# Decay matrices of a gated delta kernel: rows spread over the partitions by a DMA and subtracted on VectorE, in place of two-row products on TensorE

## The chip, the cores and the metric

The kernel runs on one core of a Trainium2 chip. The metric is the device time in microseconds (us) of one execution; lower is better. The core has TensorE (PE in the profile, with PEld for its weight loads), VectorE (DVE), ScalarE (ACT), GpSimd (POOL), and SyncE (SP), which here issues nearly all DMAs. The engines run beside each other, each through its own instructions in order, and wait for each other at semaphores.

## The reference, cut to what matters

The program is a network of two layers on 1024 tokens of width 256. The part that matters is the attention of the first layer: a gated delta rule with 16 key heads and 32 value heads, two per key head, 128 wide.

```python
beta = jax.nn.sigmoid(b)
g = -jnp.exp(A_log)[None, None, :] * jax.nn.softplus(a + dt_bias[None, None, :])
def step(state, xs):
    q_t, k_t, v_t, g_t, b_t = xs
    state = state * jnp.exp(g_t)[..., None, None]
    kv = jnp.einsum('bhk,bhkv->bhv', k_t, state)
    delta = (v_t - kv) * b_t[..., None]
    state = state + jnp.einsum('bhk,bhv->bhkv', k_t, delta)
    out = jnp.einsum('bhk,bhkv->bhv', q_t, state)
```

The kernel computes this in chunks of 128 tokens. Within a chunk the token pair (j, i), j before or at i, is weighed by exp(G_i - G_j), where G is the running sum of g over the chunk. This is the decay matrix, 128x128, one for each chunk and value head: 8 x 2 = 16 of them for a key head. It is zero where j is after i. The rest of the program (a small MLP, a second attention, a mixture of 32 experts) is not touched.

## The kernel before

The function `heads` runs the first attention as a software pipeline: step h of `STEPS` (0 to 17) prepares key head h + 1 (projection p0 to p7, the convolution's base and taps, silu, key products kk0 and kk1), builds head h (decay matrices, attention products attn0/attn1, the inverse of a triangular 128x128 matrix for each of its 16 pairs of chunk and value head), scans head h - 1 over its 8 chunks (for each chunk c: ks, qs, tx, o, su on PE; x, s, g on VectorE; qs, dl, dt, sq on ScalarE), and finishes head h - 2 (normalisation, output products out0 to out3).

The order of the work is written out by hand for each engine: `PE_PLAN`, `ACT_PLAN`, `DVE_PLAN`, `SP_PLAN` and `POOL_PLAN` hold one step as a row of names, with rows of their own for the first steps (`_FIRST`, `_SECOND`). Every engine goes through its row in order. In PE's row `p3/-1:0` is the first half of projection 3; `z0/2:1` is the second half of z0 into PSUM bank 2. The plans rest on what each piece of work waits for:

- Decay matrices: `gate_rows(h)` (L583 to L586) brings 2 x 16 rows of the running sums and their negatives from DRAM (`cum_rows`) to eight partitions of `row_from` and `row_to`, 16 KB in all, where the second of each pair of partitions or the first holds ones. `decay0` on PE (L855 to L861) makes 16 products over two partitions, which give G_i - G_j for all 16 matrices in four PSUM banks, in 32 passes. VectorE's `decay0` to `decay3` (L1348 to L1350) take min(difference, `limit`) from PSUM to `Dm`, 128x512 each; `limit` is 0 where j is at or before i and -1e30 elsewhere. ScalarE's `exp0` to `exp3` (L1082 to L1087) take the exponential in place. `attn0`, `attn1` (L1351 to L1357) and `inverse0`, `inverse1` (L1285 to L1290) multiply by `Dm`.
- Inverse: GpSimd's `solve` (`eliminate`, L1503 to L1523) inverts the 32x32 diagonal blocks by some 62 small instructions over 29 us. SP's `inverse_out` stores the result (L664 to L669), `inverse_in` loads it back with other partitions (L670 to L674). VectorE's `turn` (L1278 to L1283, three transposes) waits for that load. `y6a` on PE (L887 to L894), the first product that uses it, waits for two of the three transposes; it is a series of 32x64 products at L891 and L892. y6b, u6a, u6b, y7 and u7 follow it.
- Layout changes through DRAM, all issued by SP: `values_out` (4 stores, after VectorE's second transpose of the values, `vt1`) and `values_in` (1024 KB), `kt_out` and `kt_in` for the keys, `products_out` and `products_in` for the key products (after ScalarE's `kk1`), `outputs_out0`, `outputs_in0`, `outputs_out1`, `outputs_in1` for the outputs (after VectorE's `ot0`, `ot1`). Each load waits until its stores have landed. `w_in`, `w_z`, `w_o` bring weights.
- Scan: tx waits for x (VectorE), ks of the next chunk for s (VectorE), o for dl (ScalarE). Chunk 0 needs no x; `s0` waits for su0.
- On GpSimd `pow` and `q_root` are powers of 16 and 8 numbers per partition (2.9 and 1.6 us); `norm0` to `norm3` wait for VectorE's `factors`.

## Time and profile before

| | us |
|---|---|
| median of 3 runs | 1398.15 |
| lowest and highest run | 1395.53, 1399.49 |
| the profiled execution | 1400.72 |
| its span (first to last instruction) | 1398.9 |

| engine | busy us | share of the span |
|---|---|---|
| PE | 1289.0 | 92% |
| PEld | 875.8 | 63% |
| DVE | 969.0 | 69% |
| ACT | 790.9 | 57% |
| POOL | 753.2 | 54% |

The heads stage takes about the first 945 us: a start of some 100 us, 15 steps of about 56 us, and two steps without new heads. The page cuts the span into 40 slices and gives busy tenths for each; 9 is 90% or more:

```profile
PE   6859999999999999999999999898997899499993
PEld 3347767677677676776776767666454566346672
DVE  5848888888888888888888888755222565441554
ACT  3546867677777676777766767654322554210220
POOL 1675886867767868677677686810000000144463
PEclk9869999999999999999999999998998999699997
```

A slice is 35 us. Slices 3 to 26 are the steady steps. Matmuls are pipelined and their ends are modelled, so what one costs is read from the start of one to the start of the next. Shares of the whole span mix stages; what a change in the steps is worth is read from one step.

### The profile page before, as it was taken

The numbers are of one execution on the slowest core, as the hardware profiler recorded it, in microseconds if no ns is written. First come the engines' busy times: TensorE is split into PE (matmuls) and PEld (weight loads), VectorE is DVE, ScalarE is ACT, GpSimd is POOL, SyncE is SP. The second block draws the span as 40 slices with busy tenths as digits, with TensorE's granted clock in tenths as the row PEclk, the third lists the DMA queues.
The fourth block names the chain that finished last, engine by engine and source line by source line (L and its number), as shares of the span: only waits on it lengthen the run. The fifth ranks groups of instructions, "written<-read, shape, count | busy, mean of one in ns | idle before, by whom it ended". The sixth has DMA issues, their size and how long they took to land. (4 is left out here: it accounts for less than half of the span.)

```text
span 1398.9 us, 24967 instructions
## 1 busy us (share of the span) xinstructions
PE 1289.0 (92%) x8680; PEld 875.8 (63%) x8680; DVE 969.0 (69%) x1922; ACT 790.9 (57%) x1947; POOL 753.2 (54%) x1245
## 2 busy tenths in 40 slices
PE   6859999999999999999999999898997899499993
PEld 3347767677677676776776767666454566346672
DVE  5848888888888888888888888755222565441554
ACT  3546867677777676777766767654322554210220
POOL 1675886867767868677677686810000000144463
PEclk9869999999999999999999999998998999699997
DMA  2425355474464553744646537462007900122587
GB/s 87 113 74 118 101 146 142 98 183 118 109 170 110 153 134 97 180 114 125 166 111 154 133 95 179 116 201 68 0 1 304 275 1 1 68 72 94 125 187 186
DMA packets 233180, 171.71 MB, mean 123 GB/s; under 512 B 163746, under 2 KB 202998, under 8 KB 230240
## 3 DMA queue, kind: packets, MB, share of 16 engines
q1 hardware_dynamic: 226912, 161.59, 43.6%
q0 software_dynamic: 6144, 8.53, 3.4%
q8 instruction: 70, 1.15, 0.3%
q14 instruction: 54, 0.44, 0.1%
HBM read 104.64 MB, written 65.83 MB: 122 GB/s over the span
## 5 line engine op out<-in xcount | busy, mean ns | idle before, releaser
L723 PE MATMUL psum_banks<-main_hT,gdn_w_in 128*128 128x512 f32 x512 | 255.2, 609 | 7.4 <-DMA gdn_w_in<-in_w_in 4.1
L1227 DVE SCALAR_TENSOR_TENSOR heads_y<-psum_banks,gdn_conv_w,heads_y 128x1021 f32<-128x1021 f32 (+2 forms) x192 | 244.7, 1275 | 21.7 <-ACT heads_y L1033 17.5
L1522 POOL TENSOR_TENSOR heads_XT<-heads_XT,heads_tmp 128x126 f32<-128x126 f32 (+22 forms) x496 | 198.6, 400 | 38.9
L1519 POOL TENSOR_TENSOR heads_tmp<-heads_XT,heads_A 128x126 f32<-128x126 f32 (+22 forms) x496 | 189.6, 382 | 41.5 <-PE psum_banks L902 1.8
L723 PEld LDWEIGHTS psum_banks<-main_hT,gdn_w_in 128*128 128x128 f32 x512 | 93.5, 194 | 62.1 <-issue 52.7
L849 PE MATMUL psum_banks<-heads_w_z,main_hT 128*128 128x256 f32 x512 | 128.8, 384 | 0.0
L871 PE MATMUL psum_banks<-heads_ogT,heads_w_o 128*128 128x512 f32 x240 | 126.4, 609 | 0.2 <-issue 0.2
L849 PEld LDWEIGHTS psum_banks<-heads_w_z,main_hT 128*128 128x128 f32 x512 | 95.2, 191 | 25.2 <-issue 14.4
L1033 ACT ACTIVATE heads_y<-psum_banks,gdn_conv_w 128x1024 f32<-128x1024 f32 x64 | 71.3, 1114 | 69.3 <-PE psum_banks L723 69.0
L1057 ACT ACTIVATE heads_O<-psum_banks,heads_coef 128x128 f32<-128x128 f32 x224 | 69.6, 363 | 70.5 <-PE psum_banks L756 70.3
L1490 POOL TENSOR_TENSOR heads_og<-heads_og,heads_fac 128x512 f32<-128x512 f32 x60 | 61.2, 1041 | 80.1 <-DVE heads_fac L1294 80.1
L1248 DVE SCALAR_TENSOR_TENSOR heads_S<-heads_S,heads_coef,psum_banks 128x128 f32<-128x128 f32 x192 | 57.3, 339 | 67.9 <-PE psum_banks L773 67.8
L1933 POOL TENSOR_TENSOR main_x<-main_x,attn_probT 128x512 f32<-128x512 f32 x4 | 5.1, 1266 | 150.2 <-ACT attn_probT L1830 150.2
L767 PEld LDWEIGHTS psum_banks<-heads_X,heads_Uf 128*128 128x128 f32 x448 | 66.6, 192 | 29.2 <-issue 15.2
L1076 ACT ACTIVATE heads_junk<-heads_og 128x128 f32<-128x128 f32 x256 | 79.2, 309 | 8.6 <-DVE heads_og L1261 1.2
L753 PE MATMUL psum_banks<-heads_S,heads_kT 128*128 128x256 f32 x224 | 73.7, 411 | 5.8 <-DVE heads_S L1248 3.8
L1239 DVE SCALAR_TENSOR_TENSOR heads_X<-psum_banks,heads_coef,heads_v_s 128x128 f32<-128x128 f32 x224 | 67.9, 345 | 14.9 <-PE psum_banks L753 12.3
L2234 POOL DMA_INDIRECT expert_sum<-moe_ys,moe_place x32 | 49.4, 1542 | 51.0 <-DVE moe_ys L2312 47.8
L1061 ACT ACTIVATE heads_Dl<-psum_banks 128x256 f32<-128x256 f32 x128 | 49.0, 383 | 43.3 <-PE psum_banks L767 43.1
L767 PE MATMUL psum_banks<-heads_X,heads_Uf 128*128 128x128 f32 x448 | 69.5, 278 | 1.9 <-DVE heads_X L1239 1.9
L1065 ACT ACTIVATE heads_Dt<-psum_banks,heads_coef 128x128 f32<-128x128 f32 x224 | 70.5, 375 | 0.0
L753 PEld LDWEIGHTS psum_banks<-heads_S,heads_kT 128*128 128x128 f32 x224 | 37.3, 189 | 52.4 <-DVE heads_S L1248 27.6
(295 smaller groups left out, 3026.4 us busy)
## 6 DMA issues: line engine op xcount, KB each, us to landing
values_by_tokens<-heads_v_s SPq DMA_DIRECT2D x64, 256.0 KB, 4.2
heads_v_s<-values_by_tokens SPq DMA_DIRECT2D x16, 1024.0 KB, 5.1
outputs_by_features<-heads_ogT SPq DMA_DIRECT2D x120, 128.0 KB, 2.4
heads_ogT<-outputs_by_features SPq DMA_DIRECT2D x30, 512.0 KB, 3.8
main_w_gu<-in_w_gu SPq DMA_DIRECT2D x4, 2816.0 KB, 21.0
gdn_w_in<-in_w_in SPq DMA_DIRECT2D x16, 512.0 KB, 4.3
heads_A<-kk_blocks SPq DMA_DIRECT2D x64, 128.0 KB, 2.7
keys_by_tokens<-heads_k_tok SPq DMA_DIRECT2D x64, 128.0 KB, 4.2
```

Source lines behind the costliest of these rows:

```text
L723: ins = pe.matmul(out[:, half * 512:(half + 1) * 512], w_in[:, kd_, j * P:(j + 1) * P], hT[:, kd_, half * 512:(half + 1) * 512], start=kd_ ...
L753: pe.matmul(flat(bank_a[:, 0:2]), kT[(h - 1) % 3][:, cs], flat(S[:]), start=True, stop=True).then_inc(a_full.sem, 1)
L767: ins = pe.matmul(bank_a[:, e], Uf[old][:, e * C + c], rhs, start=True, stop=True)
L849: ins = pe.matmul(flat(bank[b][:, 2 * j:2 * j + 2]), hT[:, k, c * P:(c + 1) * P], w_z[:, k], start=k == 0, stop=k == KD - 1)
L871: ins = pe.matmul(flat(bank[b][:]), w_o[:, e, f], ogT[:, u // 2].rearrange("p q (c e) j -> p e c q j", e=HD)[:, e], start=e == 0, stop=e = ...
L1033: act.activation(y[j][:], out, ACT.Copy, scale=conv_w[:, head, j, 3:4]).then_inc(pair_base.sem, 1)
L1057: ins = act.activation(O1[:, e], bank_b[:, e], ACT.Copy, scale=coef[:, GAM, h - 1, i:i + 1])
L1065: ins = act.activation(Dt[:, e], bank_a[:, e], ACT.Copy, scale=coef[:, TAIL, h - 1, i:i + 1])
L1076: act.activation(junk[:], og[(h - 1) % 2][:, c * HD + e], ACT.Square, accum_out=ms[:, c * HD + e:c * HD + e + 1]).then_inc(sq_ready.sem, 1)
L1227: dve.scalar_tensor_tensor(y[j][:, shift:T], src[:, 0:T - shift], conv_w[:, head, j, t:t + 1], y[j][:, shift:T], ALU.mult, ALU.add).then_i ...
L1519: pool.tensor_tensor(tmp[:, 0:n, 0:m], bc_last(XT[:, 0:n, j], m), bc_mid(A0[:, j, j + 1:BLK], n), ALU.mult).then_inc(solve_step.sem, 1)
L1522: pool.tensor_tensor(XT[:, 0:n, j + 1:BLK], XT[:, 0:n, j + 1:BLK], tmp[:, 0:n, 0:m], ALU.add).then_inc(solve_step.sem, 1)
```

## The change

The running sums are kept once, in `coef[:, G_]`, and stored once, without their negatives; `diff`, `row_from`, `row_to` and their fills with ones on GpSimd are gone. `gate_rows` brings the 16 rows of a head, 8 KB, to all 128 partitions of `Dm` by one DMA, 1024 KB. VectorE's `decay0` to `decay3` then subtract G_j, a scalar per partition, and take the minimum with `limit`, in place, in four instructions of 128x128 each. PE's `decay` products and VectorE's reads of their banks go. `Dm` has two buffers. The rows of a head are refilled when the head two before it, with the same buffer, is through with `inverse1`.

The rows of all engines are written anew.

```diff
 PE_PLAN = """
-z0/2:0 tx0 z0/2:1 o0 p0/-1:0 p0/-1:1 su0 p1/-1:0 p1/-1:1 ks1 z1/1:0 qs1 z1/1:1 tx1 norm_q/2 z2/3:0 z2/3:1 o1 su1
-p2/-1:0 p2/-1:1 decay0/1 decay1/2 decay2/3 decay3/0 ks2 qs2 p3/-1:0 tx2 kk0/1 o2 su2 p3/-1:1 ks3 kk1/2 qs3 tx3 attn1/3
-o3 su3 z3/0:0 z3/0:1 p4/-1:0 p4/-1:1 ks4 qs4 p5/-1:0 tx4 p5/-1:1 o4 su4 y6a/1 y6b/2 ks5 attn0/0 qs5 tx5 u6a/1 u6b/2 o5
-su5 out0/2:0 ks6 out0/2:1 y7_0/1 p6/-1:0 p6/-1:1 qs6 tx6 out1/1:0 o6 p7/-1:0 su6 p7/-1:1 y7_1/0 u7_0/3 out1/1:1 ks7
-qs7 out2/2:0 tx7 out2/2:1 o7 out3/3:0 u7_1/0 out3/3:1
+p0/-1:0 tx0 z0/0:0 z0/0:1 p0/-1:1 o0 su0 p1/-1:0 p1/-1:1 ks1 z1/2:0 qs1 tx1 z1/2:1 z2/0:0 o1 su1 z2/0:1 norm_q/1
+p2/-1:0 p2/-1:1 ks2 p3/-1:0 qs2 tx2 p3/-1:1 o2 su2 kk0/1 kk1/3 ks3 qs3 attn0/1 tx3 z3/2:0 o3 su3 p4/-1:0 ks4 p4/-1:1
+p5/-1:0 qs4 tx4 y6a/3 y6b/0 p5/-1:1 o4 su4 u6a/1 u6b/3 ks5 z3/2:1 qs5 tx5 y7_0/0 attn1/3 y7_1/0 u7_0/1 o5 su5 p6/-1:0
+p6/-1:1 ks6 out0/0:0 qs6 tx6 out0/0:1 o6 su6 p7/-1:0 p7/-1:1 out1/3:0 out1/3:1 out2/0:0 ks7 u7_1/1 qs7 out2/0:1 tx7
+out3/2:0 o7 out3/2:1
 """
 DVE_PLAN = """
-variance kt s0 g0 vt0 x1 tap00 tap01 tap02 norm_q vt1 s1 g1 decay0 x2 decay3 decay2 decay1 s2 g2 x3 tap10 tap11
-factors tap12 g3 s3 ot0 x4 turn g4 s4 tap20 x5 scales ot1 tap21 s5 g5 tap22 attn0 x6 out0 attn1 s6 g6 tap30 x7 out1
-tap31 out2 g7 inverse0 tap32 inverse1 out3
+decay0 variance kt s0 g0 vt0 x1 tap00 vt1 tap01 tap02 s1 g1 decay1 x2 decay2 norm_q g2 s2 tap10 x3 factors tap11 tap12
+s3 g3 x4 turn attn0 ot0 s4 g4 scales x5 tap20 tap21 decay3 tap22 ot1 s5 g5 x6 attn1 inverse0 s6 out0 g6 tap30 tap31 x7
+tap32 out2 inverse1 g7 out3 out1
 """
 SP_PLAN = """
-values_out inverse_out values_in products_out inverse_in products_in outputs_out0 outputs_in0 w_z outputs_out1
-outputs_in1 kt_out kt_in w_in w_o gates
+values_out kt_out values_in inverse_out inverse_in products_out kt_in products_in outputs_out0 outputs_in0
+outputs_out1 outputs_in1 w_z gates w_in w_o
 """.split()
 POOL_PLAN = """
-pow q_root norm0 norm1 norm2 scale norm3 solve
+pow norm0 scale norm1 q_root norm2 norm3 solve
 """.split()
...
-    row_from = [a.sb(f"row_from{i}", [P, 4, P]) for i in range(2)]
-    row_to = [a.sb(f"row_to{i}", [P, 4, P]) for i in range(2)]
     limit = a.sb("limit", [P, P])
-    Dm = a.sb("Dm", [P, IT, P])
+    Dm = [a.sb(f"Dm{i}", [P, IT, P]) for i in range(2)]
...
             def gate_rows(h):
-                for sign, rows in enumerate([row_to, row_from]):
-                    src = cum_rows[sign, IT * h:IT * (h + 1)].rearrange("(g s) t -> g s t", g=4)
-                    sp.dma_start(rows[h % 2][sign:P:32], src).then_inc(s_rows[h % 2], 16)
+                src = cum_rows[IT * h:IT * (h + 1)].rearrange("i t -> (i t)").unsqueeze(0)
+                sp.dma_start(flat(Dm[h % 2][:]), src.to_broadcast([P, IT * P])).then_inc(s_rows[h % 2], 16)
...
                 elif name == "gates":
-                    b = bank_of(h, "decay3")
-                    sp.wait_ge(full[b].sem, full[b].done(h, "decay3"))
-                    gate_rows(h + 2)
+                    sp.wait_ge(uf_ready.sem, uf_ready.base(h))
+                    gate_rows(h + 1)
...
-                elif name == "decay0":
-                    for s in range(4):
-                        for g in range(4):
-                            r, out = slice(32 * g, 32 * g + 2), bank[bank_of(h, f"decay{g}")]
-                            ins = pe.matmul(out[:, s], row_from[par][r, s], row_to[par][r, s], start=True, stop=True)
-                            if s == 3:
-                                ins.then_inc(full[bank_of(h, f"decay{g}")].sem, 1)
...
+                if name.startswith("decay"):
+                    if u == 0:
+                        dve.wait_ge(s_rows[par], 16 * (h // 2 + 1))
+                    for i in range(4 * u, 4 * u + 4):
+                        ins = dve.scalar_tensor_tensor(Dm[par][:, i], Dm[par][:, i], coef[:, G_, h, i:i + 1], limit[:], ALU.subtract, ALU.min)
+                    ins.then_inc(decay_ready.sem, 1)
+                    return
...
-                elif name.startswith("decay"):
-                    dve.wait_ge(full[b].sem, full[b].done(h, name))
-                    dve.tensor_tensor(Dm[:, 4 * u:4 * u + 4], bank[b][:], bc_mid(limit[:], 4), ALU.min).then_inc(free[b].sem, 1)
...
-            dve.tensor_copy(cum_t[:, 0], bank_b[:, 2:4]).then_inc(s_ct, 1)
-            dve.tensor_scalar(cum_t[:, 1], bank_b[:, 2:4], -1.0, None, ALU.mult).then_inc(s_ct, 1)
+            dve.tensor_copy(cum_t, bank_b[:, 2:4]).then_inc(s_ct, 1)
...
-            for i in range(2):
-                pool.memset(row_from[i][:], 1.0).then_inc(s_ones, 1)
-                pool.memset(row_to[i][:], 1.0).then_inc(s_ones, 1)
```

ScalarE's row changes too: exp0 to exp3 still stand between `z2` and `z3`. The rows of the first two steps are new in the same way; SP's row of step 0 keeps its order, without `gates`.

## Rows read from the trace of the kernel before

**Rows 1.** Stretches: start:end, length; busy PE, PEld, DVE, ACT, POOL; PEclk, DMA share, GB/s
```profile
486.22:542.32 56.10, 55.82 (x435) 39.40 (x434) 47.76 (x90) 40.03 (x103) 41.96 (x74) 1.00 0.54 135
502.70:506.10 3.40, 3.40 (x24) 2.82 (x23) 2.47 (x6) 2.71 (x11) 2.82 (x2) 1.00 1.01 223
```

**Rows 2.** Timeline of PE: first small product of two neighbouring steps
```profile
462.39 0.27 PE L891 MATMUL psum_banks<-heads_Xh,heads_kneg 32*64 32x64 f32 x1
...
518.50 0.27 PE L891 MATMUL psum_banks<-heads_Xh,heads_kneg 32*64 32x64 f32 x1
```

**Rows 3.** Timeline of PE: items of one step; start, duration, "x4" counts passes
```profile
486.22 1.03 PE L849 MATMUL psum_banks<-heads_w_z,main_hT 128*128 128x256 f32 x4
487.09 0.61 PE L767 MATMUL psum_banks<-heads_v_s,heads_Uf 128*128 128x128 f32 x4
...
488.84 1.88 PE L723 MATMUL psum_banks<-main_hT,gdn_w_in 128*128 128x512 f32 x4
490.56 0.59 PE L773 MATMUL psum_banks<-heads_Dt,heads_k_tok 128*128 128x256 f32 x2
```

**Rows 4.** Timeline of PE around the decay products of that step
```profile
499.11 1.88 PE L723 MATMUL psum_banks<-main_hT,gdn_w_in 128*128 128x512 f32 x4
500.92 1.17 PE L859 MATMUL psum_banks<-heads_row_to,heads_row_from 2*128 2x128 f32 x32
502.03 0.70 PE L753 MATMUL psum_banks<-heads_S,heads_kT 128*128 128x256 f32 x2
```

**Rows 5.** Timeline of VectorE: taps, value turn, scan pair, decays, inverse turn
```profile
494.06 3.92 DVE L1227 SCALAR_TENSOR_TENSOR heads_y<-psum_banks,gdn_conv_w,heads_y 128x1021 f32<-128x1021 f32 x3
...
498.45 1.24 DVE L1308 STREAM_TRANSPOSE heads_v_s<-heads_y 128x1024 f32<-128x1024 f32 x1
...
502.76 0.61 DVE L1239 SCALAR_TENSOR_TENSOR heads_X<-psum_banks,heads_coef,heads_v_s 128x128 f32<-128x128 f32 x2
503.29 1.28 DVE L1350 TENSOR_TENSOR heads_Dm<-psum_banks,heads_limit 128x512 f32<-128x512 f32 x2
...
516.10 2.17 DVE L1283 STREAM_TRANSPOSE heads_Xh<-heads_Uf 32x512 f32<-32x512 f32 x3 [0.35 <-DMA heads_Uf<-inverse_blocks]
```

**Rows 6.** Timeline of SP: transfers of that step; start and length of issues
```profile
499.71 2.90 SPq L636 DMA_DIRECT2D values_by_tokens<-heads_v_s  x4
502.72 2.47 SPq L669 DMA_DIRECT2D inverse_blocks<-heads_XT  x2
506.12 0.34 SPq L640 DMA_DIRECT2D heads_v_s<-values_by_tokens  x1
...
511.28 3.18 SPq L674 DMA_DIRECT2D heads_Uf<-inverse_blocks  x4
...
528.12 4.07 SPq L623 DMA_DIRECT2D keys_by_tokens<-heads_k_tok  x4
534.68 1.71 SPq L628 DMA_DIRECT2D heads_k_tok<-keys_by_tokens  x4
```

**Rows 7.** Timeline of SP at the start: a 1024 KB load, stores behind it
```profile
67.64 0.34 SPq L640 DMA_DIRECT2D heads_v_s<-values_by_tokens  x1
68.09 2.08 SPq L573 DMA_DIRECT2D kk_blocks<-heads_kneg  x4
...
73.83 1.71 SPq L580 DMA_DIRECT2D heads_A<-kk_blocks  x4
```

**Rows 8.** All DMA issues by line, KB each, median us to landing
```profile
heads_v_s<-values_by_tokens SPq DMA_DIRECT2D x16, 1024.0 KB, 5.1
...
inverse_blocks<-heads_XT SPq DMA_DIRECT2D x32, 128.0 KB, 4.2
...
heads_v_s<-in_mlp_w SPq DMA_DIRECT2D x1, 1024.0 KB, 9.4
```

**Rows 9.** Timelines of VectorE and GpSimd: instructions with only SBUF operands
```profile
1202.79 1.75 DVE L1911 SCALAR_TENSOR_TENSOR main_rows<-attn_probT,attn_rms_rstd,main_lend 128x256 f32<-128x256 f32 x2
...
1202.59 1.27 POOL L1933 TENSOR_TENSOR main_x<-main_x,attn_probT 128x512 f32<-128x512 f32 x1 [2.77 <-ACT attn_probT L1830]
```

More of the change, by code:

```diff
@@ L212 @@
[L212 to L213 removed]
+p0/-1:0 p0/-1:1 p1/-1:0 p1/-1:1 p2/-1:0 p2/-1:1 p3/-1:0 p3/-1:1 norm_q/3 p4/-1:0 kk0/2 kk1/3 p4/-1:1 p5/-1:0 p5/-1:1
+p6/-1:0 p6/-1:1 p7/-1:0 attn0/1 p7/-1:1 y6a/3 y6b/0 u6a/2 u6b/0 attn1/1 y7_0/3 y7_1/2 u7_0/3 u7_1/2
 """
 PE_SECOND = """
[L217 to L218 removed]
@@ L282, in belongs @@
         return h == HK + 1
[L283 removed]
+    if name == "w_in":
         return h + 2 < HK
+    if name == "gates":
+        return 0 < h < HK - 1
     if name == "w_z":
@@ L790, in product_waits @@
                     pe.wait_ge(act_ready.sem, act_ready.done(h, "sq"))
-                elif name == "decay0":
-                    pe.wait_ge(s_rows[par], 32 * (h // 2 + 1))
-                    for g in range(1, 4):
-                        more = free[bank_of(h, f"decay{g}")]
-                        wait(pe, more, more.ahead(h, f"decay{g}"))
                 elif name.startswith("flip"):
```

79 lines of the change are left out of this document (36 added, 43 removed).

## The prediction

> **What bounds the kernel now.** I read three views in this order. The stretches view says which engine is full: over one whole head step of the steady part PE is busy for 55.82 of 56.10 us at the full granted clock (1.00, so 2.4 GHz), VectorE for 47.76, ScalarE 40.03, GpSimd 41.96 [rows 1]. The first small product of one step and that of the next stand 56.11 us apart [rows 2], so a step takes 56.1 us. The timeline of PE then shows why PE is full: every item starts when the passes before it are through. In the list of waits PE itself hardly appears; the other engines wait for it. So steps 1 to 15 last as long as PE's row, and a change pays there only by what it takes out of that row, and only if nothing new holds an item of it. In step 0 the row of PE is not the limit; GpSimd's elimination and the transfers around it are.
>
> I count time from the first product of the step of the traced example, 486.22 [rows 3]. In these terms y6a, the first product that needs the inverse blocks, starts at 518.50 - 486.22 = 32.3 [rows 2, 3].
>
> **What leaves PE.** The 16 two-row products of a head are 32 passes. They start at 500.92 and the next item at 502.03, which is 1.11 us. The four passes before them started at 499.11 and alone need 1.72 (488.84 to 490.56), so PE could have gone on at 500.83: 0.09 is lost at the entry. The scan product behind lasts 0.70 where such a product lasts 0.59 elsewhere: 0.1 more [rows 3, 4]. Together 1.3 us a head. PE's row becomes 56.1 - 1.3 = 54.8 us in each of the steps 1 to 15, or 15 x 1.3 = 19.5 us in all, if every other item still comes in time. Step 0 gains nothing from it.
>
> **What VectorE gets.** Out go four evacuations of 128x512, 1.28 us for two, 2.5 for four. In come 16 instructions of 128x128 with a scalar per partition. The nearest row is the pair of the scan, same operation and shape with one operand in PSUM: 0.61 us for two [rows 5]. Lower bound: the rate of the old form, 2.5 for all 16; upper bound: 16 x 0.305 = 4.9. I take 4.3, since back to back the second of such a pair adds less than half. So VectorE grows by 1.8 us (0 to 2.4), from 47.8 to 49.6 of 54.8. It has room in sum, but its row is served in order, and any delay ahead of a scan update reaches PE.
>
> The new instructions read only SBUF. Where such an instruction met one of GpSimd, two of 128x256 took 1.75 us, and they lie across a GpSimd instruction of 1.27 that started 0.2 before [rows 9]. So one waits for the other. By the order of the rows only decay0 meets the elimination of GpSimd; decay1 and decay2 come when GpSimd works on the small power and then waits for `factors`, decay3 between its scaling of A0 and its next large one. I count 0.2 us for each of decay0's four, and they stand before s0, which waits for su0 at 4.8 anyway: nothing on the path.
> The Trainium skill (SBUF — State Buffer, SBUF: two separate sides) says that this pair of ports is an exclusive lock, held for the whole instruction by whoever starts first. The rows agree. By that rule alone the power on GpSimd, too, would hold the lock: rival 3.
>
> **What ScalarE and SP get.** The four Exp keep shape and place between the same kinds of table; no cost. The new load brings 1024 KB where 16 KB were brought. It goes after `outputs_in1` and `w_z`: `ot1` stands some 40 us into VectorE's row and its store needs about 5 more, so near 46 (an estimate). It must land by 54.8 + 1.4 = 56.2, when `decay0` opens VectorE's next row. Nearest rows: 5.1 us in median for 1024 KB from DRAM, 9.4 for a load of that size with others ahead [rows 8]. It lands at 51 to 56: in time, barely at the upper end. `w_in` stands behind it; from p7 to the next p0 PE has six halves of 0.86, four scan items of 0.43 and u7_1, some 8 us. No cost. Refilling after the last use (the wait on `uf_ready`) is long satisfied.
>
> **What is moved, and what comes late.** This decides the case. The new rows move y6a forward. Of what stood before it in PE's row these are now behind it: half of a z pair (0.87 for four passes), one half of a p pair (0.86), o4 (0.44, half of a z's time for half its columns), su4 (0.43), and the decay products (1.30) are gone [rows 3, 4]. y6a's place is 32.3 - 3.9 = 28.4. It needs the inverse blocks loaded and two of the three turns, 2 x 0.72 of 2.17 [rows 5]. So the load must have landed by 26.9.
>
> When can it? I follow SP's row, which is served in order.
> 1. The values' turn vt1 ends today at 498.45 + 1.24, 13.5 in the step. Its place in front of tap01, tap02 and norm_q now: today three taps start at 494.06 and take 3.92; it can start after the first of them, at 495.4, and end at 496.6 = 10.4 [rows 5]. It can't be earlier, since tap00 hangs on p1, which ends at 6.5 in both rows. The 1.1 us of decay0 are absorbed by the wait for su0.
> 2. `values_out` starts at 10.4, issues for 2.9, and has landed after 506.12 - 499.71 = 6.4: 16.8 [rows 6].
> 3. `kt_out` is now next: issues from 13.3, 4.07 long, so SP is free at 17.4. Alone it lands 534.68 - 528.12 = 6.6 after its start. Behind the values it lands at 19.9 if the queue keeps its pace and at 16.8 + 6.6 = 23.4 if nothing overlaps; I take 20.3.
> 4. `values_in`, 1024 KB, issued at 17.4. Alone 5.1 [rows 8]. Behind the keys: 20.3 + 4.4 = 24.7 (between 22.5 and 28). The 4.4 is 1024 KB at the 223 GB/s that were moved with a DMA share of 1.01 [rows 1], 4.7, a little less for its long rows.
> 5. `inverse_out`, issued at 17.8 for 2.5 us. Today it stands in front of `values_in`. If it does not wait for what is ahead of it, it is there 4.2 after its second issue (18.9): 23.1. If it does, it lands about 1.3 behind `values_in`: 26.0.
> 6. `inverse_in`: today from 511.28 to 516.10, when VectorE's turn is released: 4.8 [rows 5, 6]. It lands at 27.9 to 32.3, and I take 30.5.
>
> Does a store wait for a large load ahead of it? At the start it does:  four stores of 32 KB issued from 68.09 to 70.17 behind a load of 1024 KB let SP go on only at 73.83 [rows 7], 3.7 us after the last issue, while the keys, four times as much, let it go on 534.68 - 532.19 = 2.5 after theirs [rows 6]. So I take the late end.
> The Trainium skill (DMA: Bandwidth & Descriptors, Queues, rings and completion order) says that descriptors of one queue start in order on each DMA engine. All of these transfers are SP's. It speaks against the new order, and it would give the late end, the sum below.
>
> So y6a starts at 30.5 + 1.45 + 0.05 = 32.0 in place of 28.4: PE waits 3.6 us (bounds 1.0 and 5.4). Behind it VectorE, held in front of `turn`, has some 27 us of its row left for PE's 26.4; I add 0.4 for places where it then lags (0 to 1). The step is 54.8 + 3.6 + 0.4 = 58.8 us, 2.7 more than today. Steps 1 to 14 run this order: 14 x 2.7 = +38 us. Step 15 and the start I set at zero (-3 to +3): in the start one small copy and four fills go, and twelve decay instructions meet the elimination of step 0.
>
> The profiled execution took 1400.72 us, 1398.9 of them span; the median of the runs is 1398.15. 1398 + 38 = **1436 us**. Its own range, from stalls of 2.1 to 5.2: 1415 to 1458.
>
> **The rivals.**
> 1. *The gain arrives.* The queue overlaps its transfers better than I read; the inverse lands by 27.2, PE waits at most 0.4 a step. For it: step 5's early end; alone each of these transfers lands within 4 to 7 us. Then 1398 - 19.5 + 14 x 0.4 = **1384** (1379 to 1393). It decides where the load lands before 28.2 in the step.
> 2. *It cancels.* The load lands near 28.2 and PE waits 1.3 a step: **1398** (1392 to 1405).
> 3. *The port.* The new instructions are held by all that GpSimd does, the power included. Then decay1 waits up to some 3 us just before x2, PE waits for tx2 some 3.5: 58.3 a step, +2.2 x 15, **1431**. Against it: the powers are calculation more than reading; no row shows them holding VectorE. It does not add to the queue's stall, which starts at vt1, ahead of decay1.
> 4. *The spread rows come late.* Each us beyond 10.1 from issue to landing delays decay0, and PE from about 1.5 us on. With 12 us, +1 a step: **1399** on a clean row, **1451** with the stall. Reading the same 8 KB for 128 partitions is in no row.
> 5. *It doesn't do what it says*: PE's item costs less than 1.3, as entry and exit losses stay at the neighbours. Lower bound 1.11 a head, 3 us in all; within every range above.
>
> **How the numbers follow.** Queue stall 0.50; gain arrives 0.26; it cancels 0.13; port 0.07; late rows 0.04. Of "it cancels" I give 0.04 to faster, 0.07 to the same and 0.02 to slower. Faster by over 0.3% (4.2 us, about what a measurement of this kernel can tell from no change): 0.26 + 0.04 = 0.30. Same: 0.07. Slower: 0.50 + 0.07 + 0.04 + 0.02 = 0.63. The range must reach into the faster case: 1382 to 1456.
>
> **What would show it.** Right: a step of 58 to 60 us; PE idle 3 to 4 us before the line of y6a with VectorE's turn as releaser; VectorE's turn released by the DMA into heads_Uf; SP's inverse store issued behind the values' load, and 6 us or more from there to `inverse_in`. No passes of the two-row products, sixteen small VectorE instructions of 0.3 us a head. Wrong: a step near 55 us with PE full, and the turn not waiting for a DMA (rival 1); long new instructions on VectorE beside GpSimd's power (rival 3); `decay0` released by a DMA (rival 4).

## The result

The changed kernel takes 1489.45 us (median of 4 runs, 1485.42 to 1494.75), the kernel before beside it 1398.82 (4 runs, 1395.53 to 1399.83). The ratio is 1.066 (95% interval 1.061 to 1.070): 91 us slower, where I had forecast 38. Its profiled execution took 1494.75, of which 1492.9 are span; the spans differ by 94.0.

The page of the changed kernel, its utilization rows for PE and the granted clock:

```profile
PE   6677999999899999999999999978798899689994
...
PEclk9869999999999999899998999889998999889997
```

A slice is 37 us here. PE's row looks nearly as full as before. The second row has 8 in four slices of the steady steps (17, 22, 26 and 27), where before had 9 in all of them; a mean over 37 us hides most of what was lost, and the stretches below show it.

The next rows are stretches (start:end, length; busy PE, PEld, DVE, ACT, POOL; PEclk, DMA share, GB/s). A step is counted here from its first tx to the next one. First, for before, steps 2 to 14 as one stretch:

```profile
150.13:880.17 730.04, 728.97 (x5644) 513.80 (x5643) 625.73 (x1159) 525.80 (x1356) 549.57 (x958) 1.00 0.54 134
```

Then, for the changed kernel, the same thirteen steps; one step of them; and out of that step PE's wait before y6a, what comes right behind it, and what comes then:

```profile
169.21:962.76 793.55, 751.34 (x5225) 532.27 (x5224) 661.92 (x1311) 520.69 (x1351) 546.51 (x950) 0.94 0.55 140
...
533.00:593.41 60.41, 57.74 (x403) 40.87 (x402) 50.64 (x103) 39.94 (x105) 42.33 (x74) 0.94 0.55 142
560.57:563.24 2.67, 0.00 (x1) 0.00 (x1) 1.43 (x3) 1.01 (x4) 2.67 (x3) 1.00 0.58 104
563.24:570.40 7.16, 7.16 (x136) 5.36 (x136) 4.80 (x12) 3.04 (x5) 1.38 (x2) 0.52 0.86 210
570.40:577.00 6.60, 6.60 (x74) 5.82 (x63) 5.91 (x12) 5.54 (x15) 5.93 (x6) 1.00 0.29 83
```

A mean step is 793.55 / 13 = 61.04 us instead of 730.04 / 13 = 56.16. In 560.57 to 563.24 PE does nothing. In the 7.16 us behind it PE is busy all the time, at a granted clock of 0.52, so nearly all at 1.2 GHz, and then it is back at 1.00. Before, the clock was 1.00 over all thirteen steps (the stretch above).

The 94.0 us by which the spans differ, split at the first tx of each step: 8.0 up to the first one (106.97 against 99.00), 11.1 in step 1 (62.25 against 51.13), 63.5 in steps 2 to 14, 11.2 in step 15 (58.56 against 47.33), 0.2 in all that follows. The stages behind the heads are untouched.

The timeline of PE in the example step of the changed kernel (start, duration, and the idle time in front with its releaser), which answers to [rows 2, 3]:

```profile
535.17 1.02 PE L719 MATMUL psum_banks<-main_hT,gdn_w_in 128*128 128x512 f32 x2
536.03 0.61 PE L774 MATMUL psum_banks<-heads_Dl,heads_At 128*128 128x128 f32 x4
...
559.96 0.61 PE L763 MATMUL psum_banks<-heads_X,heads_Uf 128*128 128x128 f32 x4
563.24 0.27 PE L875 MATMUL psum_banks<-heads_Xh,heads_kneg 32*64 32x64 f32 x1 [2.67 <-DVE heads_Xh L1266]
...
565.00 2.08 PE L719 MATMUL psum_banks<-main_hT,gdn_w_in 128*128 128x512 f32 x2
566.86 1.06 PE L774 MATMUL psum_banks<-heads_Dl,heads_At 128*128 128x128 f32 x4
```

y6a waits 2.67 us for VectorE's turn. The two passes of projection behind it last 2.08 where the same two last 1.02 elsewhere in the step, and the four of an o item 1.06 instead of 0.61. That is the half clock, read from durations.

VectorE in that step, which answers to [rows 5]: decay0, decay1, turn.

```profile
533.54 2.03 DVE L1315 SCALAR_TENSOR_TENSOR heads_Dm<-heads_Dm,heads_coef,heads_limit 128x128 f32<-128x128 f32 x4
...
546.11 1.13 DVE L1315 SCALAR_TENSOR_TENSOR heads_Dm<-heads_Dm,heads_coef,heads_limit 128x128 f32<-128x128 f32 x4
...
561.75 2.17 DVE L1266 STREAM_TRANSPOSE heads_Xh<-heads_Uf 32x512 f32<-32x512 f32 x3 [3.13 <-DMA heads_Uf<-inverse_blocks]
```

SP in that step, which answers to [rows 6]: start and length of the issues.

```profile
542.43 3.10 SPq L633 DMA_DIRECT2D values_by_tokens<-heads_v_s  x4
545.63 4.19 SPq L620 DMA_DIRECT2D keys_by_tokens<-heads_k_tok  x4
549.86 1.15 SPq L637 DMA_DIRECT2D heads_v_s<-values_by_tokens  x1
551.12 2.00 SPq L666 DMA_DIRECT2D inverse_blocks<-heads_XT  x2
557.78 1.90 SPq L671 DMA_DIRECT2D heads_Uf<-inverse_blocks  x4
```

The inverse is issued at 551.12, 1.3 us behind the load of the values, and `inverse_in` can go out only at 557.78, when both stores have landed. The medians to landing of all DMA issues say the same for all steps; they answer to [rows 8], where these stores took 4.2 and the load of the values 5.1:

```profile
heads_v_s<-values_by_tokens SPq DMA_DIRECT2D x16, 1024.0 KB, 6.8
...
inverse_blocks<-heads_XT SPq DMA_DIRECT2D x32, 128.0 KB, 6.3
```

Over steps 2 to 14 the list of waits (engine, line, releaser: us in total, times, longest) has in the changed kernel:

```profile
DVE heads_Xh L1266 <- DMA heads_Uf<-inverse_blocks: 47.0, 13, 4.6
...
PE psum_banks L875 <- DVE heads_Xh L1266: 41.1, 13, 4.1
```

So 13 waits of 3.2 us in the mean before y6a, for a turn that waits for the load.

### The profile page after: what moved, and what is told of

It is laid out like the page before. It is cut to its first block and busy times, and to the rows that moved or that the text cites. A ratio compares the mean times of both kernels' runs of the same rounds, so it can differ in the third digit from the quotient of the medians.

```text
span 1492.9 us, 24081 instructions
## 1 busy us (share of the span) xinstructions
PE 1322.7 (89%) x8168; PEld 900.0 (60%) x8168; DVE 1017.9 (68%) x2113; ACT 786.9 (53%) x1947; POOL 750.2 (50%) x1241
## 5 line engine op out<-in xcount | busy, mean ns | idle before, releaser
L719 PE MATMUL psum_banks<-main_hT,gdn_w_in 128*128 128x512 f32 x512 | 271.7, 644 | 17.2 <-DVE heads_y L1210 11.4
L1505 POOL TENSOR_TENSOR heads_tmp<-heads_XT,heads_A 128x126 f32<-128x126 f32 (+22 forms) x496 | 193.0, 389 | 42.2 <-PE psum_banks L886 2.5
L1508 POOL TENSOR_TENSOR heads_XT<-heads_XT,heads_tmp 128x126 f32<-128x126 f32 (+22 forms) x496 | 193.0, 389 | 38.9
L719 PEld LDWEIGHTS psum_banks<-main_hT,gdn_w_in 128*128 128x128 f32 x512 | 97.0, 201 | 88.7 <-issue 59.3
L840 PE MATMUL psum_banks<-heads_w_z,main_hT 128*128 128x256 f32 x512 | 133.0, 393 | 0.8 <-ACT heads_Uf L1122 0.8
L855 PE MATMUL psum_banks<-heads_ogT,heads_w_o 128*128 128x512 f32 x240 | 118.3, 594 | 1.4 <-DMA heads_ogT<-outputs_by_features 1.1
L1315 DVE SCALAR_TENSOR_TENSOR heads_Dm<-heads_Dm,heads_coef,heads_limit 128x128 f32<-128x128 f32 x256 | 94.2, 428 | 0.0
L1487 POOL TENSOR_TENSOR heads_v_s<-heads_v_s,heads_k_root 128x2048 f32<-128x2048 f32 x16 | 58.2, 3640 | 42.2 <-DMA heads_v_s<-values_by_tokens 42.2
L769 PE MATMUL psum_banks<-heads_Dt,heads_k_tok 128*128 128x256 f32 x224 | 74.4, 417 | 3.0 <-ACT heads_Dt L1049 3.0
L875 PE MATMUL psum_banks<-heads_Xh,heads_kneg 32*64 32x64 f32 x256 | 28.4, 292 | 51.5 <-DVE heads_Xh L1266 51.5
```

Source lines behind the costliest of these rows:

```text
L719: ins = pe.matmul(out[:, half * 512:(half + 1) * 512], w_in[:, kd_, j * P:(j + 1) * P], hT[:, kd_, half * 512:(half + 1) * 512], start=kd_ ...
L769: pe.matmul(flat(bank_a[:, 0:2]), k_tok[old][:, c], flat(Dt[:]), start=True, stop=True).then_inc(a_full.sem, 1)
L840: ins = pe.matmul(flat(bank[b][:, 2 * j:2 * j + 2]), hT[:, k, c * P:(c + 1) * P], w_z[:, k], start=k == 0, stop=k == KD - 1)
L855: ins = pe.matmul(flat(bank[b][:]), w_o[:, e, f], ogT[:, u // 2].rearrange("p q (c e) j -> p e c q j", e=HD)[:, e], start=e == 0, stop=e = ...
L1315: ins = dve.scalar_tensor_tensor(Dm[par][:, i], Dm[par][:, i], coef[:, G_, h, i:i + 1], limit[:], ALU.subtract, ALU.min)
L1505: pool.tensor_tensor(tmp[:, 0:n, 0:m], bc_last(XT[:, 0:n, j], m), bc_mid(A0[:, j, j + 1:BLK], n), ALU.mult).then_inc(solve_step.sem, 1)
```

## The experiments

All times are medians, ratios against the kernel before on the same chip with their 95% intervals. In the diffs only the plan rows that differ are shown. The forecast of each experiment stands in front of what it gave.

### The inverse ahead of the large transfers

```diff
 SP_PLAN
-values_out kt_out values_in inverse_out inverse_in products_out kt_in products_in outputs_out0 ...
+values_out inverse_out values_in inverse_in kt_out products_out kt_in products_in outputs_out0 ...
```

> The changed kernel, with SP's row alone altered in steps 1 to 15: values_out, inverse_out, values_in, inverse_in, kt_out in place of values_out, kt_out, values_in, inverse_out, inverse_in. The changed kernel (1489) has in each steady step a PE wait of 3.2 us before y6a, and right behind it 6.8 to 10.2 us at half the granted clock (563.4 to 570.3 in one step), which costs half of that, about 3.7. Theory A (the clock falls because PE stood idle, and both come from SP's order): with the inverse blocks ahead the load lands near 26 in the step, y6a does not wait, the clock stays at 1.00 in the steady steps, each step is 54 to 55 us, and the time is 1489 - 14 x (3.2 + 3.7) = 1392 (1375 to 1405). Rival B (the clock falls from the load on the chip, whatever PE did before): only the wait goes, 1489 - 14 x 3.2 = 1444, with the half-clock stretches still there. Rival C (the wait hangs on something other than SP's order, GpSimd's elimination for one): no change, 1489.

Measured: 1430.4, ratio 1.021 (1.018 to 1.024). 59 us of the 91 are gone by an order of DMA issues alone, 13 more than the waits before y6a had been (41.1 in steps 2 to 14 and 4.85 in step 15). Stretch of steps 2 to 14, and from the list of waits there:

```profile
164.96:910.53 745.57, 726.45 (x5225) 514.97 (x5224) 655.76 (x1312) 521.64 (x1350) 544.49 (x948) 0.98 0.57 149
```

```profile
DVE heads_rnd L1253 <- ACT heads_nd L1026: 27.6, 13, 3.3
ACT heads_nd L1026 <- DMA heads_A<-kk_blocks: 27.2, 13, 3.3
...
PE psum_banks L763 <- DVE heads_X L1222: 19.1, 13, 2.7
```

In these steps y6a never waits now; it starts 27.5 after the first tx in each of them. But 38 us are missing from the forecast, and the waits say where: ScalarE's `norms` (L1026) wait for the key products' load, VectorE's `scales` (L1253) for ScalarE, the x behind it is late, and PE waits up to 2.7 us. The kernel falls between theories A and B. What speaks for A is where the clock was lost: of the thirteen steps those with a PE wait of 1.4 to 2.7 us had a half-clock stretch, and those with less had none, with one exception at 1.61.

### More work in the wait

```diff
                 elif name == "y6a":
+                    if h > 0:
+                        wait(pe, free[b], free[b].ahead(h, name))
+                        for _ in range(6):
+                            pe.matmul(flat(bank[b][:]), hT[:, 0, 0:P], hT[:, 0, 0:512], start=True, stop=True)
                     pe.wait_ge(xh_ready.sem, xh_ready.done(h, "2"))
```

> The changed kernel with more work: in steps 1 to 15 PE makes six products of 128x512 (2.6 us) that nobody reads, into y6a's own bank, just ahead of its wait for VectorE's turn. SP's order and the landing of the inverse blocks stay. Theory A (idle PE brings the clock down): y6a starts where it did, 0 to 1.5 us of idle is left, the clock stays at 1.00 in most steps, and the step loses the 3.7 us that half clock cost: 1489 - 14 x 3.7 = 1437 (1430 to 1460). Rival B (the clock falls from the load, not from idle): the wait is filled and nothing is won, 1489 to 1500, with half-clock stretches as before or longer ones. What would surprise under A: a clock that falls all the same with 1 us of idle left.

> As the kernel with six products in the wait, but three. Six took 5.2 us, not the 2.6 I had counted (one of 128x512 is two records of 0.43), so they pushed y6a back by some 2 us past the landing; still the clock stayed at 1.00 in steps 3 to 14 and the kernel was 13 us faster than without them. Three are 2.6 us and end about where the mean wait of 3.2 ends. Theory A (idle PE brings the clock down): 0 to 1.5 us of idle is left, the clock stays at 1.00, the step is 54.3 + 3.2 = 57.5, and the time 1489 - 13 x 3.6 = 1442 (1436 to 1455). Rival B (the longer idle is not what brings the clock down): half clock in the steps as before, and 1476 to 1489.

Measured: 1476.6 with six (ratio 1.055, 1.053 to 1.057), 1462.7 with three (1.048, 1.045 to 1.050); each is against 1489.45 without any. Steps 2 to 14 with six, then with three:

```profile
176.66:954.64 777.98, 777.91 (x5381) 532.63 (x5380) 654.44 (x1307) 519.91 (x1347) 544.06 (x948) 1.00 0.56 143
```

```profile
170.62:936.72 766.10, 750.65 (x5304) 518.51 (x5303) 653.34 (x1308) 520.66 (x1347) 544.27 (x948) 0.99 0.57 145
```

This is the experiment that decides. PE makes more products, SP's order is that of the change, and the kernel is 13 and 27 us faster. With six, PE is hardly idle in these steps (777.91 of 777.98 busy) and the clock stays at full (1.00 against 0.94). Rival B, a clock that falls from load, is out: the load is higher. With three, ten of the twelve steps 3 to 14 keep the clock; in the two others PE stood still for 1.87 and 2.14 us. Both times were above their forecasts, 1437 and 1442. I had mis-sized six products at 2.6 us; they are 5.2, and the 2.6 more in fifteen steps are the 39 us missing. With three, I had reckoned PE's row at 54.3, and it is 54.9 (below), and waits of up to 1.9 before y6a were left.

### The queue's part alone, in the kernel before

```diff
 SP_PLAN
-values_out inverse_out values_in products_out inverse_in products_in outputs_out0 outputs_in0 w_z outputs_out1
-outputs_in1 kt_out kt_in w_in w_o gates
+values_out kt_out values_in inverse_out inverse_in products_out products_in outputs_out0 outputs_in0 w_z outputs_out1
+outputs_in1 kt_in w_in w_o gates
```

> The kernel before (1398), with SP's row of the steady steps alone altered: kt_out moved up behind values_out, and inverse_out behind values_in, as the change orders them; all else, TensorE's decay products too, is that of before. It is the queue's part of the change alone. In the changed kernel the inverse load landed 19.2 us after the end of vt1. Here vt1 ends 13.5 in the step, so the load lands at 32.7, and after 1.45 of turn y6a can start at 34.2 where its place is 32.3: a PE wait of 1.9 us. Theory A (idle PE brings the clock down): 1398 + 14 x 1.9 = 1425 if 1.9 us of idle is too little to bring the clock down, and about 1398 + 14 x (1.9 + 3.4) = 1472 if it is enough. Rival D (the order of the queue is harmless by itself, and it is the new instructions or the 1024 KB load that hold the inverse): 1398.

Measured: 1517.9, ratio 1.084 (1.081 to 1.087). From its waits in steps 2 to 14 and their stretch:

```profile
PE psum_banks L891 <- DVE heads_Xh L1283: 27.9, 13, 3.4
PE psum_banks L871 <- issue: 20.0, 10, 3.7
```

```profile
168.37:1004.18 835.81, 772.95 (x5643) 544.50 (x5642) 629.33 (x1159) 525.84 (x1356) 553.34 (x972) 0.94 0.48 117
```

27.9 / 13 = 2.1 us before y6a, as forecast (1.9), and the half clock with it (0.94). The rest is one more wait, before the output products at L871 (in the example of step 3, `ot0` was through at 262.5, but SP, waiting for the inverse and the key products, stored the outputs only at 270.17; their load landed at 278.76 and L871 started at 278.85), and 15 us once, before y6a of step 1, where kt is late in VectorE's row and SP's `kt_out` waits for it ahead of all else. So the whole was 46 us above the forecast of 1472; what answers to the change is the wait before y6a with its half clock. With nothing of the new mechanism in it, an order of this kind alone makes the kernel before slower than the change did. Rival D is out.

### The new mechanism alone, in the rows of before

PE's rows of before without the decay products, VectorE's with the new decays in the places of the evacuations, the row load last in SP's row:

```diff
 DVE_PLAN
-variance kt s0 g0 vt0 x1 tap00 tap01 tap02 norm_q vt1 s1 g1 decay0 x2 decay3 decay2 decay1 s2 g2 x3 tap10 ...
+variance kt s0 g0 vt0 x1 tap00 tap01 tap02 norm_q vt1 s1 g1 decay0 x2 decay1 decay2 decay3 s2 g2 x3 tap10 ...
```

> The change's way to make the decay matrices, with the rows of before for every engine: TensorE's decay products are struck out of its row, VectorE's decay0 to decay3 stand (in that order) where its four evacuations stood, the load of the rows is the last of SP's row. It is the other part of the change alone. My sum before the run: TensorE's row loses 1.3 us a head; the changed kernel's steps, less its wait and its lost clock, give 54.3, which would be 1.8. So if nothing new is late: 1398 - 15 x 1.3 = 1379 to 1398 - 15 x 1.8 = 1371, and the clock at 1.00. Rival E (VectorE's sixteen new instructions hold its row, since 5.4 us where 2.5 were, some of it beside GpSimd, delay the scan updates): PE waits for VectorE in each step, and the time is 1390 to 1420. Rival D (the 1024 KB load crowds the queue, so w_in comes late): PE waits at p0.

And the same with only one of four instructions, which leaves out three quarters of the differences:

```diff
-                    for i in range(4 * u, 4 * u + 4):
+                    for i in range(4 * u, 4 * u + 1):
```

> The old rows with the new decay mechanism, but VectorE makes only one of the four instructions of each decay; three quarters of the differences are left out. It takes 3.4 us of VectorE's work and its delays out of each step and leaves PE's row as it is. Theory A (VectorE's lateness keeps half of PE's gain): steps of 54.8 to 54.9, 1396.3 - 15 x 0.65 = 1386.5. Rival B (PE's row itself is 55.5): 1395 to 1397.

Measured: 1396.25 with all (ratio 0.999, 0.998 to 1.000), 1388.3 with a quarter (0.994, 0.992 to 0.996). One steady step of each, all first:

```profile
599.96:655.49 55.53, 55.16 (x403) 38.54 (x402) 49.69 (x102) 40.35 (x104) 43.78 (x74) 1.00 0.60 155
```

```profile
205.48:260.28 54.80, 54.74 (x403) 38.56 (x402) 46.73 (x90) 40.40 (x104) 41.93 (x74) 1.00 0.60 157
```

The first was forecast at 1371 to 1379 if nothing came late; it is rival E, VectorE holding its row, that holds. With most of VectorE's new work taken away a step is 54.80, to the hundredth what the prediction's first step gave; seven of the thirteen steps are that long, the others longer (up to 59.21, where PE waited 0.87 for S and 1.77 before an output product). With all of it, a step is 55.53, so 0.73 of the 1.3 that leave PE are paid back. Where, VectorE's timeline and PE's show:

```profile
615.44 3.23 DVE L1316 SCALAR_TENSOR_TENSOR heads_Dm<-heads_Dm,heads_coef,heads_limit 128x128 f32<-128x128 f32 x12
...
619.24 0.70 PE L750 MATMUL psum_banks<-heads_S,heads_kT 128*128 128x256 f32 x2 [0.32 <-DVE heads_S L1232]
```

Twelve instructions in a row, 3.23 us, stand in front of s2, and PE waits for S; the pair after such a wait lasts 0.70 instead of 0.59 besides. These are 0.43 of the 0.73. Twice I spread the instructions:

```diff
 DVE_PLAN, first try (with ScalarE's exp0 moved behind dt2)
-s1 g1 decay0 x2 decay1 decay2 decay3 s2 g2 x3 tap10
+s1 g1 x2 decay0 decay1 decay2 s2 g2 x3 decay3 tap10
 DVE_PLAN, second try
-s1 g1 decay0 x2 decay1 decay2 decay3 s2 g2 x3 tap10
+s1 g1 decay0 x2 decay1 decay2 s2 g2 x3 decay3 tap10
```

> The old rows with the new decay mechanism took 1396.3 and a steady step of 55.52: PE gained 0.58 a head where I had counted 1.3. In its step PE waits 0.32 for s2 (twelve of the sixteen instructions stand in front of it and take 3.2 us) and 0.15 for x2 (behind decay0). Here VectorE's row has x2 ahead of decay0, three decays in the gap before s2, the last one behind x3; ScalarE's exp0 goes behind dt2, so that it does not hold them. Theory A (the 0.7 that is missing is VectorE's lateness): steps of 54.8 to 55.1, 1396.3 - 14 x 0.5 = 1389 (1386 to 1392). Rival B (the products cost PE only some 0.6 net, since its neighbours now pay their own entry losses): 1395 to 1397.

> The old rows with the new decay mechanism (1396.3), VectorE's row changed little: decay0 x2 decay1 decay2 s2 g2 x3 decay3, so eight instructions stand between x2 and s2 instead of twelve; ScalarE's row stays. In the kernel with x2 ahead of decay0 and exp0 later the 0.32 us before ks3 went, but ScalarE's dl3 then came late and PE waited 0.43 before o3, so nothing was won. With a quarter of the instructions PE's step was 54.80, just what I had counted. Theory A: the wait for s2 goes (2.2 us of decays end before su2 does), nothing is put on ScalarE, and steps are 55.1 to 55.3: 1396.3 - 14 x 0.3 = 1392 (1389 to 1395). Rival B (decay3 behind x3 makes the taps or x4 late): 1396 to 1400.

Measured: 1398.0 (ratio 1.001, 1.000 to 1.002) and 1397.7 (0.999, 0.998 to 1.001). No gain. The timelines of PE, first try and second:

```profile
403.01 0.71 PE L775 MATMUL psum_banks<-heads_Dl,heads_At 128*128 128x128 f32 x4 [0.43 <-ACT heads_Dl L1046]
```

```profile
237.95 1.55 PE L720 MATMUL psum_banks<-main_hT,gdn_w_in 128*128 128x512 f32 x3 [0.27 <-DVE heads_y L1211]
```

Each time the wait before ks3 went and another came, for ScalarE's dl3 once and for VectorE's taps once. The times are those of the two rivals B (the first 1 us above it). But the reason that the first of them gives, a PE row that is itself 0.7 longer, does not fit the 54.80 with a quarter of the instructions.

### The other items of the queue

```diff
 SP_PLAN, keys behind the outputs' first half
-values_out inverse_out values_in inverse_in kt_out products_out kt_in products_in outputs_out0 outputs_in0 ...
+values_out inverse_out values_in inverse_in products_out products_in outputs_out0 outputs_in0 kt_out kt_in ...
 SP_PLAN, products_in ahead of kt_in only
-values_out inverse_out values_in inverse_in kt_out products_out kt_in products_in outputs_out0 outputs_in0 ...
+values_out inverse_out values_in inverse_in kt_out products_out products_in kt_in outputs_out0 outputs_in0 ...
```

> The inverse-first kernel with one more edit in SP's row: products_out, products_in, outputs_out0 and outputs_in0 go ahead of kt_out and kt_in. In the inverse-first kernel y6a no longer waits, but in steps 2 to 13 PE stood still for 0.5 to 2.7 us before a tx, because VectorE's scales waited up to 3.3 us for ScalarE's norms and those for the loads from kk_blocks, which SP issued behind the keys; the clock fell after the longer ones. Theory A (the same queue, one step on): the products land 6 us earlier, the tx wait goes, and with it the clock loss of these steps. The idle beyond 0.5 a step is 11.5 us and the lost clock 15.4, so 1430 - 27 = 1403 (1398 to 1410), steps of 55.4. It stays above before because of the start and steps 1 and 15. Rival B (it is the shorter row itself that is too tight for VectorE): PE goes on waiting before tx, 1420 to 1430. Rival C (the keys come late in their turn): PE waits at the first scan items of the next step, 1410 to 1430.

> The changed kernel's rows with SP's row as values_out, inverse_out, values_in, inverse_in, kt_out, products_out, products_in, kt_in, outputs_out0 and on: from the inverse-first kernel (1430), kt_in and products_in change places. There PE waited before a tx in steps 2 to 13, as the key products came late to ScalarE's norms; with products_in, outputs_out0 and outputs_in0 ahead of all of the keys that wait went, but the second outputs (outputs_out1) then stood behind 9 us of key transfers, and PE waited 3.4 to 5.6 us before an out product, at 1506. Here outputs are ahead of nothing new. Theory A (each item of SP's row has a due time, and only the order is at fault): the products land some 2 to 3 us earlier than in the inverse-first kernel, the wait before tx falls from 1.5 us in the mean to under 0.7, which is too little to bring the clock down, steps are 55.4 to 55.8, and the time is 1430 - 24 = 1406 (1400 to 1415). What is left above before is the start (+8), steps 1 and 15. Rival B (no order of this row serves all): 1420 or more, with a new wait somewhere.

Measured: 1505.7 (ratio 1.076, 1.073 to 1.079) and 1405.3 (1.004, 1.002 to 1.006). The first was a miss, by 100 us. Its waits in steps 2 to 14:

```profile
PE psum_banks L855 <- DMA heads_ogT<-outputs_by_features: 61.8, 13, 5.6
```

I had placed 9 us of key transfers in front of `outputs_out1`, which was due 5 us before they ended, and PE waited 4.8 us a step for an output load. The second came out as forecast (1406). Its steps 2 to 14:

```profile
164.59:882.19 717.60, 713.67 (x5226) 502.78 (x5224) 653.68 (x1309) 520.92 (x1347) 545.74 (x949) 1.00 0.60 155
```

717.60 / 13 = 55.20, clock 1.00; PE is busy for 713.67 of it, so its row is 713.67 / 13 = 54.9. All other rows, VectorE's with its sixteen instructions too, are those of the change. 84 of the 91 us came from the order of one engine's row.

### The start and step 1

The changed kernel's timelines of VectorE (decay3 of step 1; decay1 of step 2) and of GpSimd (the multiplication of 128x2048 in step 1; a power in step 2):

```profile
133.50 4.38 DVE L1315 SCALAR_TENSOR_TENSOR heads_Dm<-heads_Dm,heads_coef,heads_limit 128x128 f32<-128x128 f32 x4
...
182.33 1.13 DVE L1315 SCALAR_TENSOR_TENSOR heads_Dm<-heads_Dm,heads_coef,heads_limit 128x128 f32<-128x128 f32 x4
```

```profile
133.31 3.64 POOL L1487 TENSOR_TENSOR heads_v_s<-heads_v_s,heads_k_root 128x2048 f32<-128x2048 f32 x1 [12.96 <-DMA heads_v_s<-values_by_tokens]
...
181.85 2.91 POOL L1528 TENSOR_TENSOR heads_rs<-heads_var,heads_minus_half 128x16 f32<-128x16 f32 x1
```

Four instructions that take 1.13 alone take 4.38 beside the multiplication, and end at 137.88, 0.93 after it does. Beside the power they take 1.13.

```diff
 DVE_SECOND, first try
-s3 g3 attn0 decay3 x4
+s3 g3 decay3 attn0 x4
 DVE_SECOND, second try
-s2 decay2 x3 ... s3 g3 attn0 decay3 x4
+s2 decay2 decay3 x3 ... s3 g3 attn0 x4
```

> The same with one swap in VectorE's row of step 1 alone: decay3 ahead of attn0. In the changed kernel decay3 of step 1 took 4.38 us instead of 1.13, beside GpSimd's multiplication of 128x2048 (3.64 us), and PE waited 2.98 for the x behind it; in the inverse-first kernel it took 2.57 and ended 0.93 after that multiplication did. The reads of attn0, of which one operand is in PSUM, took their usual 1.41 beside it. Theory A (an instruction of VectorE with all operands in SBUF and one of GpSimd hold each other off): decay3 takes 1.13, before the multiplication begins, the wait for x in step 1 goes, and the kernel is 1.5 to 4 us faster than its neighbour without the swap. Rival B (the 4.38 came of something else, its data or the queue): decay3 is as long as before, and nothing is won.

> The kernel of 1405 with decay3 of step 1 right behind decay2, at about 124, well ahead of GpSimd's multiplication of 128x2048 (130.8 to 134.4). Where I had put it directly ahead of attn0 it started at 130.3, still met that multiplication, and took 4.51 us. Theory A (instructions of the two engines with all operands in SBUF exclude each other for their whole length): decay3 takes 1.13, PE's 1.29 us wait for the x behind it goes, x3 is up to 1.1 later, and the time is 1400 to 1405. Rival B (decay3 is slow in step 1 for another reason): it takes 2.5 or more here too.

Measured: 1404.0 (ratio 1.005, 1.003 to 1.007) and 1405.2 (1.007, 1.004 to 1.009), both within noise of the kernel without the swap (1405.3). In the first the decay started at 130.29, the multiplication at 130.41, and the four took 4.51. In the second both decays lie well ahead of it:

```profile
124.59 2.19 DVE L1315 SCALAR_TENSOR_TENSOR heads_Dm<-heads_Dm,heads_coef,heads_limit 128x128 f32<-128x128 f32 x8
```

Eight take 2.19, so decay3 is 1.1 again. So the two hold each other off. That it cost the kernel something that could be told apart is not shown: in the second try PE's 1.29 us wait for x was gone, and a wait of 1.79 us before a su item stood in its place.

Last, steps 0 and 1 with the rows of before for PE, ScalarE and VectorE, and then SP's row of step 1 as before too:

```diff
-    return [name for name in (SP_PLAN if h else SP_FIRST) if belongs(h, name)]
+    return [name for name in (SP_PLAN if h > 1 else SP_SECOND if h else SP_FIRST) if belongs(h, name)]
```

> The kernel of 1405 (the changed rows with SP's row in the order inverse, keys out, products, keys in), but steps 0 and 1 of TensorE, ScalarE and VectorE have the rows of before, with the decay products struck out and VectorE's decays in their places. In the kernel of 1405 the steady steps 2 to 14 take 717.6 us against 730.0 before, 12.4 less, and this is eaten by the start (its first tx at 106.7 against 99.0), step 1 (57.9 against 51.1) and step 15 (52.4 against 47.3). With the old rows everywhere the first tx came at 102.6 and step 1 took 52.1. Theory A (the loss at the start is the new rows of steps 0 and 1, turn far behind in VectorE's and decay3 beside GpSimd's multiplication): first tx at 103, step 1 at 52 to 54, so 1405 - 3.7 - 5 = 1396 (1392 to 1400). Rival B (the start is lost to the new mechanism, its 1024 KB loads and twelve instructions beside GpSimd's elimination, whatever the rows): 1402 to 1407.

> The kernel with the old rows in steps 0 and 1 (1407), and now SP's row of step 1 is that of before as well. In that kernel step 1 took 62.3 us: VectorE's kt stood late in the old row of step 1, SP's kt_out waited for it, and the key products stood behind kt_out, so VectorE's scales waited 6.3 us and PE 5.0 before u6a. Theory A (again an item of the queue that waits holds those behind it): scales do not wait, step 1 is 52 to 54 us as with the old rows everywhere, and the time is 1407 - 8 - 2 = 1397 (1393 to 1400), so 0 to 4 us below before. Rival B (the old rows of step 1 do not fit the new rows of step 2, whatever the queue): 1403 or more.

Measured: 1407.0 (ratio 1.008, 1.007 to 1.010) and 1397.8 (1.000, 0.998 to 1.001). In the first, kt stood late in VectorE's old row, and SP held the key products behind it: VectorE's `scales` waited 6.3 us, and step 1 took 62.3. In the second step 1 is 54.0, as forecast, but step 2 then has a PE wait of 3.12 before a tx, with a half-clock stretch behind it. Steps 3 to 14 are at 55.0 us in the mean.

No version beats the kernel before by more than can be told. What the steady steps gain (12 us in the kernel of 1405.3) goes at the start, in step 1 and in step 15.

## Why the prediction was wrong in size

*What leaves PE, 1.3 us a head.* Right: 54.80 (quarter of the decays) against 56.10.

*VectorE, 4.3 us and 0.8 for decay0.* Near in size: 2.03 + 3 x 1.13 = 5.4 a head. "Nothing on the path" held in the rows of the change (54.9) and failed in the old rows, where 0.7 of the 1.3 are paid back.

*The load of the rows in time.* Right: the median was 7.2 us to landing, and no VectorE decay waited for it.

*The queue.* Right, and near in each of its terms. In the example step, counted from p0 at 532.14, y6a's place is 560.57 - 532.14 = 28.4 (forecast 28.4), the load released turn at 29.6 (30.5), and y6a started at 31.1 (32.0). The mean wait was 3.2 (3.6).

*Behind the wait, 0.4 us.* This is the step that failed. The prediction says "VectorE, held in front of `turn`, has some 27 us of its row left for PE's 26.4; I add 0.4 for places where it then lags". The sum let PE go on at full clock after each wait; the clock was neither in it nor among the rivals. What came instead: 61.04 - 54.9 - 3.2 = 3.0 us a step. From the other side, the kernel with six products is 15.6 us shorter in steps 2 to 14 although it does 13 x 5.16 = 67.1 more and has no 41.1 of waits: 15.6 + 67.1 - 41.1 = 41.6, or 3.2 a step. So each wait was paid twice, once standing and once at half clock. In the sum 0.4 should have been 3.0: 2.6 us a step more, less 0.4 for the shorter wait: 61.04 against 58.8, or 29 us in thirteen steps.

The trace of before did hold a warning, in a stretch that I had not read, behind the heads: PE idle for 3.1 us, then busy at half clock, then at full (stretches as above).

```profile
1053.45:1056.57 3.12, 0.00 (x0) 0.00 (x0) 0.00 (x0) 0.75 (x2) 0.00 (x0) 0.50 0.01 3
1056.57:1061.10 4.53, 4.47 (x6) 1.92 (x7) 0.32 (x1) 0.59 (x1) 0.34 (x1) 0.50 0.65 172
1061.10:1066.00 4.90, 4.90 (x13) 2.26 (x12) 2.29 (x1) 1.47 (x4) 0.00 (x0) 1.00 1.00 428
```

The clock had fallen before this idle time began, at 1050.9; ahead of that PE had been idle from 1048.31 to 1050.50. So these rows show half clock behind idle time and busy work at half clock, but not which of the idle stretches brought it.

The Trainium skill (TensorE: Matmul & The Clock Gate, HAM oscillation — how this bites in real kernels) describes this: a TensorE that waits for a DMA between two groups of products is set back to the lower clock, and the products behind the wait are slow too. The traces agree, with a clock of 0.52 behind 2.67 us of idle time. The prediction should have had it as a rival or in the sum.

*Start and step 15 at zero, step 1 like any other.* Wrong by 8.0, 11.2 and 11.1 - 2.7 = 8.4, together 28 us: the other half of the miss (29 + 28 against 94.0 - 37.8 = 56). The start: the first tx is at 99.0 before and at 99.6 with a quarter of the decays, which has the 1024 KB loads too, so these cost it next to nothing. In the five kernels with the old rows of step 0 and all decays it is at 102.6 to 105.5, 104.3 in the mean: some 5 us for VectorE's decays, twelve of which take 6.0 us beside the elimination and stand in front of the values' second transpose. In the eight with the new rows it is at 105.8 to 109.2, 107.0 in the mean; what in these rows costs the remaining 2.7 us was not separated. Step 1 has no wait before y6a at all, though the prediction gave it the same 2.7: PE waits 2.98 us there for an x and 2.50 before a su item, and the clock is at half for 6.8 us. Step 15 went from 58.6 to 52.4 with the queue's order, so over half of its loss is the same wait and clock (4.85 us before y6a); the rest stays open.

*The rivals.* The gain did not arrive. The port: the powers hold nothing (1.13 beside a power of 2.91), as argued; but a large multiplication does, and I had looked only at what lies beside the decays in the steady steps. "It does not add to the queue's stall" missed that a second loss can be the stall's own echo.

## What to carry to other kernels

Give a wait of a TensorE that is otherwise full the price of its length and, from some 2 us on, that of the half-clock work behind it as well; here that doubled it. A row of DMA issues is a schedule like any engine's: write down for each item when its source is ready and when its reader wants it before moving one, since here one order of the same sixteen items gave 1405, another 1430, 1489 or 1506. And when an engine is relieved of work, its neighbours must have been ahead of it to begin with; VectorE, 48 of 56 us busy, gave back over half of the gain (0.73 of 1.3).
